# Second token phase of a conv-attention hybrid block: the partner product of q replaced by an exchange matrix on q's fp16 halves

## The reference

```python
# layer 0: attention over channels-first tokens, with a bias table, added to x
x  = x + w_out @ attention(w_qkv @ layernorm_c(x))
# layer 1: attention with relative embeddings, 8 heads of width 32
proj = layernorm(t) @ W + b                 # q, k, v of each head
qk = einsum('bhqd,bhkd->bhqk', q, k)
emb = sinusoidal_embeddings(length, 32)[q - k + length - 1]
qe = einsum('bhqd,qkd->bhqk', q, emb)
weights = softmax((qk + qe) / sqrt(32))
t = t + weights @ v
# layer 2: gates by sinkhorn, top-k routing to 8 experts
t = t + experts(layernorm(t))
```

## Time and profile before

| | us |
|---|---|
| median of 3 runs | 2913.53 (2912.02 to 2914.46) |
| profiled execution | 2905.21 |
| its span | 2903.4 |
| PE busy | 2553.8 (88%) |
| DVE busy | 2023.3 (70%) |
| POOL busy | 1971.1 (68%) |
| ACT busy | 1401.9 (48%) |

### The profile page before, as it was taken

How to read it: one execution, slowest core, us unless ns; L and a number is a source line. 1 busy time by engine, 2 the same in 40 slices (tenths; PEclk the granted TensorE clock), 3 DMA queues, 4 the chain that set the end, 5 groups by cost and what they waited for, 6 DMA issues and landing times. The chain is left out here.

```text
span 2903.4 us, 47732 instructions
## 1 busy us (share of the span) xinstructions
PE 2553.8 (88%) x18726; PEld 872.9 (30%) x18726; DVE 2023.3 (70%) x3094; ACT 1401.9 (48%) x2558; POOL 1971.1 (68%) x767
## 2 busy tenths in 40 slices
PE   6899999999999999879989999999999999761355
PEld 2563222222222222245542222222222222240244
DVE  3575877878878778757766777777777777578134
ACT  4345555555555555422225555555555555440012
POOL 2124888888888888743447887878878878630763
PEclk8999999999999999989999999999999999875568
DMA  3993123221122211268654222223212232260347
GB/s 81 253 227 120 49 49 78 62 52 49 48 74 66 52 48 49 53 230 266 218 184 110 48 63 48 63 80 77 63 48 63 62 90 53 89 188 9 91 122 243
DMA packets 239569, 284.41 MB, mean 98 GB/s; under 512 B 65014, under 2 KB 172790, under 8 KB 236014
## 3 DMA queue, kind: packets, MB, share of 16 engines
q1 hardware_dynamic: 228848, 256.12, 32.5%
q0 software_dynamic: 6144, 16.85, 1.9%
q10 hardware_dynamic: 4352, 8.39, 0.8%
HBM read 171.59 MB, written 110.47 MB: 97 GB/s over the span
## 5 line engine op out<-in xcount | busy, mean ns | idle before, releaser
L843 POOL TENSOR_TENSOR room_af<-room_af 128x2048 f32<-128x2048 f32 x160 | 725.7, 4536 | 164.4 <-ACT room_af L815 150.2
L1191 POOL TENSOR_TENSOR bias<-bias 128x2048 f32<-128x2048 f32 x160 | 724.6, 4529 | 148.5 <-ACT bias L1163 134.6
L978 DVE TENSOR_REDUCE row_min_kf<-PS 128x1 f32<-128x1024 f32 x532 | 627.5, 1220 | 267.4 <-PE PS L970 265.9
L625 DVE CUSTOM_DVE_ANT_0 PS<-PS,bias 128x1024 f32<-128x1024 f32 x532 | 644.2, 1241 | 161.3 <-PE PS L613 148.3
L1163 ACT ACTIVATE bias<-PS 128x512 f32<-128x512 f32 x1024 | 557.1, 597 | 412.2 <-PE PS L1089 411.1
L815 ACT ACTIVATE room_af<-PS 128x512 f32<-128x512 f32 x1024 | 555.7, 595 | 398.2 <-PE PS L737 398.2
L1089 PE MATMUL PS<-stacks_kf 128*128 128x512 f16 x2048 | 533.1, 383 | 7.7 <-PEq L86 7.6
L730 PE MATMUL PS<-QS_af,KS_af 128*128 128x512 f16 x1024 | 334.1, 387 | 11.1 <-PEq L86 4.5
L1089 PEld LDWEIGHTS PS<-stacks_kf 128*128 128x128 f16 x2048 | 156.9, 97 | 448.3 <-ACT bias L1163 292.3
L763 PE MATMUL PS<-room_af,V_af 128*32 128x512 f32 x2048 | 272.7, 605 | 0.3 <-ACT room_af L815 0.3
L1109 PE MATMUL PS<-bias,V_kf 128*32 128x512 f32 x2048 | 272.7, 604 | 0.0
(11 more groups left out here) (180 smaller groups left out, 2847.0 us busy)
## 6 DMA issues: line engine op xcount, KB each, us to landing
stacks_kf<-query_key_halves SPq DMA_DIRECT2D x119, 256.0 KB, 7.0
query_key_halves<-bias SPq DMA_DIRECT2D x32, 768.0 KB, 3.8
query_key_halves<-room_af SPq DMA_DIRECT2D x32, 512.0 KB
KS_af<-query_key_halves SPq DMA_DIRECT2D x51, 256.0 KB, 4.9
QS_af<-query_key_halves SPq DMA_DIRECT2D x51, 256.0 KB, 6.9
V_kf<-values SPq DMA_DIRECT2D x9, 1024.0 KB, 10.5
V_af<-values SPq DMA_DIRECT2D x17, 512.0 KB, 8.9
stacks_kf<-query_key_halves SPq DMA_DIRECT2D x68, 128.0 KB, 9.1
```

The lines of the kernel that those rows point to most:

```text
L625: nc.vector.tensor_tensor_reduce(out=max_ps[n % len(max_ps)], in0=max_ps[n % len(max_ps)], in1=bias_h[:, g * HG + j, z:z + N], scale=-1.0, ...
L843: nc.gpsimd.tensor_tensor(acc[:, u % 2], so_far, prob[:, n % PR], ALU.add).then_inc(acc_ok, 1)
L978: nc.vector.tensor_reduce(row_min[:, m:m + 1], max_ps[n % len(max_ps)], AX.X, ALU.min).then_inc(max_read, 1)
L1191: nc.gpsimd.tensor_tensor(acc[:, u % 2], so_far, prob[:, n % PR], ALU.add).then_inc(acc_ok, 1)
```

## The change

PE makes the partner of q no longer from the layer-normed tokens but from q's own halves in `stg`: two matmuls with a 128x128 exchange matrix `swap` as weights, one for the high and one for the low half, in place of six. Since those halves hold the bias, DVE's step for part 1 of the rotation multiplies only (`tensor_tensor` in place of `scalar_tensor_tensor`). PE must wait for both halves of q of the group. The order of a round is changed, so that other steps stand between q and its partner. `w1_p` shrinks to 3C columns, the bias table `bcol` to four columns, and the four weight jobs for w1q take 256, 256, 512 and 512 columns. DVE writes `swap` in the setup by two copies out of the identity.

```diff
--- before.py
+++ after.py
@@ -61,13 +61,14 @@
 
         wqkv_p = sb("wqkv_p", [P, 2, KT, 3 * C], F16)
         wout_p = sb("wout_p", [P, 2, KT, C], F16)
-        w1_p = sb("w1_p", [P, 2, KT, 4 * C], F16)
+        w1_p = sb("w1_p", [P, 2, KT, 3 * C], F16)
         gate_p = sb("gate_p", [P, 2, KT, E], F16)
         gates = sb("gates", [P, B * NT * E], F32)
         idf = sb("idf", [P, P], F32)
         ones = sb("ones", [P, P], F32)
         bvb = sb("bvb", [P, C], F32)
-        bcol = sb("bcol", [P, 6], F32)
+        bcol = sb("bcol", [P, 2 * G], F32)
+        swap = sb("swap", [P, P], F16)
         eps = sb("eps", [P, 1], F32)
         eyes = sb("eyes", [P, W], F16)
         bias = sb("bias", [P, H, ZU * W], F32)
@@ -166,9 +167,8 @@
                     bc = [("bc", c, 0)] if c < NCH else []
                     qk = [("qk", u, m) for m in range(NQ)] if u >= 0 else []
                     v = [("v", u, m) for m in range(NV)] if u >= 0 else []
-                    last_qk = NQ - 1
                     steps = (qk[0:2] + tp + qk[2:] + v[0:1] + bc + v[1:],
-                              qk[0:3] + proj + qk[3:last_qk] + tp + qk[last_qk:] + v[0:1] + bc + v[1:])[kind]
+                              qk[0:1] + qk[2:3] + proj + qk[1:2] + qk[3:4] + tp + qk[5:6] + qk[4:5] + v[0:1] + bc + v[1:])[kind]
                     some = [("max", n, job) for n, job in jobs[:PER]] if u > early.after else []
                     jobs = jobs[len(some):]
                     for n, name in enumerate(steps):
@@ -336,11 +336,18 @@
                                     pe.wait_ge(high, u + 1)
                                     pe.wait_ge(low, u + 1)
                                 w, g = m % (NQ // G), m // (NQ // G)
-                                last = product(ps, wp, w * C + g * P, lambda s, k: (xh, xl)[s][:, u % 2, k, :])
+                                if kind == 1 and w == 1:
+                                    s = u * G + g
+                                    pe.wait_ge(q_high, 2 * s + 1)
+                                    pe.wait_ge(q_low, 2 * s + 1)
+                                    for h in range(2):
+                                        last = nc.tensor.matmul(ps, swap[:], stg[:, u % 2, g, h, :], start=(h == 0), stop=(h == 1))
+                                else:
+                                    last = product(ps, wp, (w != 0) * C + g * P, lambda s, k: (xh, xl)[s][:, u % 2, k, :])
                             else:
                                 for t in range(2):
                                     last = tokens_first(u, ps[:, t * C:(t + 1) * C],
-                                                        slice((2 * m + t) * P, (2 * m + t + 1) * P), NQ // G * C)
+                                                        slice((2 * m + t) * P, (2 * m + t + 1) * P), 2 * C)
                             last.then_inc(full, 1)
 
                     @block.scalar
@@ -381,7 +388,7 @@
                                 elif w != 1:
                                     act.wait_ge(full, n + 1)
                                     nc.scalar.activation(stg[:, u % 2, g, 2 * w, :], bank(name), ACT.Identity,
-                                                         bias=bcol[:, w * G + g:w * G + g + 1]).then_inc(q_high, 1)
+                                                         bias=bcol[:, w // 2 * G + g:w // 2 * G + g + 1]).then_inc(q_high, 1)
                                 if kind == 1 and m == NQ // G:
                                     turned_high(u, 0)
                             elif what == "v" and kind == 0:
@@ -484,16 +491,15 @@
                                     nc.vector.scalar_tensor_tensor(out=lo, in0=bank(name), scalar=(QS, 1.0)[w] / SC, in1=hi,
                                                                    op0=ALU.mult, op1=ALU.subtract).then_inc(q_low, 1)
                                     continue
-                                b_ = bcol[:, w * G + g:w * G + g + 1]
+                                b_ = bcol[:, w // 2 * G + g:w // 2 * G + g + 1]
                                 if w < 2:
                                     dve.wait_ge(full, n + 1)
                                     if s >= 2:
                                         dve.wait_ge(added, s - 1)
                                     tok = place(u)[1]
                                     if w == 1:
-                                        nc.vector.scalar_tensor_tensor(out=tf[:, s % 2, 1, :], in0=bank(name), scalar=b_,
-                                                                       in1=rots[:, 1, tok], op0=ALU.add,
-                                                                       op1=ALU.mult).then_inc(turned, 1)
+                                        nc.vector.tensor_tensor(tf[:, s % 2, 1, :], bank(name), rots[:, 1, tok],
+                                                                ALU.mult).then_inc(turned, 1)
                                 if w != 1:
                                     dve.wait_ge(q_high, 2 * s + w // 2 + 1)
                                     nc.vector.scalar_tensor_tensor(out=lo, in0=bank(name), scalar=b_, in1=hi, op0=ALU.add,
@@ -1220,7 +1226,7 @@
                 def ssem(name):
                     return es.enter_context(nc.semaphore(name))
 
-                w_sum = KT * (3 * C + C + 4 * C)
+                w_sum = KT * (3 * C + C + 3 * C)
                 room, keys, queries = early.rooms[0], *early.scratch
                 chunks, w_st = room[:, 0:4 * KT * CH], room[:, 4 * KT * CH:4 * KT * CH + w_sum + 256]
                 rel = zf[0:2, 0:SIDE * SIDE]
@@ -1237,7 +1243,7 @@
 
                 WL = []
                 off = 0
-                for src, dst, cols in ((wqkv, wqkv_p, 3 * C), (wout, wout_p, C), (w1q, w1_p, 4 * C)):
+                for src, dst, cols in ((wqkv, wqkv_p, 3 * C), (wout, wout_p, C), (w1q, w1_p, 3 * C)):
                     WL.append((src, dst, w_st[:, off:off + KT * cols].rearrange("p (k n) -> p k n", k=KT)))
                     off += KT * cols
                 small = w_st[:, off:off + 256]
@@ -1252,7 +1258,7 @@
                 cen = room[:, first:first + 2 * P].rearrange("p (i n) -> p i n", i=2)
 
                 WJ = []
-                for n, cols in ((2, slice(0, CH)), (2, slice(CH, 2 * CH)), (0, slice(0, CH)), (0, slice(CH, 3 * C))):
+                for n, cols in ((2, slice(0, C)), (2, slice(C, 3 * C)), (0, slice(0, CH)), (0, slice(CH, 3 * C))):
                     scale = -QS * W1S if n == 2 and cols.start == 0 else (WS, WS, W1S)[n]
                     for k in range(KT):
                         WJ.append((WL[n][1], WL[n][2], k, cols, scale, n == 0))
@@ -1374,8 +1380,11 @@
                                 dve.wait_ge(cst_in, 48)
                                 with nc.allow_low_precision(reason="each sum has a single one among zeros"):
                                     nc.vector.reduce_sum(eyes[:], bass.AP(idf, W - 1, [[P, P], [-1, W], [W, ROWS]]), AX.X)
-                                nc.vector.tensor_scalar(bcol[:, 0:4], bcol[:, 0:4], -QS * W1S, None, ALU.mult)
-                                nc.vector.tensor_scalar(bcol[:, 4:6], bcol[:, 4:6], W1S, None, ALU.mult)
+                                nc.vector.tensor_scalar(bcol[:, 0:G], bcol[:, 0:G], -QS * W1S, None, ALU.mult)
+                                nc.vector.tensor_scalar(bcol[:, G:2 * G], bcol[:, G:2 * G], W1S, None, ALU.mult)
+                                halves_of = [t_.rearrange("p (h t d) -> p h t d", t=2, d=D // 2) for t_ in (swap[:], idf[:])]
+                                for t in range(2):
+                                    nc.vector.tensor_copy(halves_of[0][:, :, t, :], halves_of[1][:, :, 1 - t, :])
                             if j == len(WJ):
                                 dve.wait_ge(w_high, len(WJ) + 1)
                                 nc.vector.scalar_tensor_tensor(out=wout_p[:, 1], in0=WL[1][2], scalar=WS, in1=wout_p[:, 0],
@@ -1892,10 +1901,8 @@
 
     w1 = a["L1_attn_W"].reshape(C, H, 3, D)
     b1 = a["L1_attn_b"].reshape(H, 3, D)
-    swap = np.concatenate([np.arange(D // 2, D), np.arange(D // 2)])
-    w1q = con(np.concatenate([w1[:, :, 0].reshape(C, C), w1[:, :, 0][:, :, swap].reshape(C, C),
-                              w1[:, :, 1].reshape(C, C), w1[:, :, 2].reshape(C, C)], axis=1))
-    cols = [b1[:, 0].reshape(-1, 128), b1[:, 0][:, swap].reshape(-1, 128), b1[:, 1].reshape(-1, 128)]
+    w1q = con(np.concatenate([w1[:, :, i].reshape(C, C) for i in range(3)], axis=1))
+    cols = [b1[:, 0].reshape(-1, 128), b1[:, 1].reshape(-1, 128)]
     b1cols = con(np.concatenate(cols, axis=0).T)
     b1v = con(b1[:, 2].reshape(-1))
```

## The result

| us | before | after |
|---|---|---|
| median of 4 timed runs each | 2912.93 (2912.02 to 2914.46) | 2893.52 (2891.83 to 2896.32) |
| profiled execution | 2905.21 | 2896.32 |
| its span | 2903.4 | 2894.5 |
| PE busy | 2553.8 | 2541.5 |

The account below looks back on a forecast made before the run. A loop from `bc` to `bc` through PE, ACT and DVE was taken as the bound: 14 rounds x 1.52 = 21.3 us, last rounds 0, setup 1.7, together 23.0, so 2913.5 becomes 2890.5 us; own range 2886 to 2896, 8-in-10 range 2885 to 2899.

Parts of the forecast that it names:

- The loop: Second token phase, `bc` to `bc` through PE, ACT and DVE: rounds 17.15 to 15.63 and 15.59 to 14.07, 21.3 us.
- leg 2: From m3's end to the next `bc`, set by DVE: L494 for m4 leaves it, 6.67 to 6.01 us.
- leg 1: PE's work from `bc` to m3's end: m1 sheds 0.86 us, 10.48 to 9.62.
- PE's sum as the bound: Rival, second token phase: PE's wait doesn't grow and both matmul savings count, 29.3 us with setup, 2884.2; chance 0.07.
- The saving hidden: Rival, first leg: DVE's sequence sets it, m1's 0.86 becomes a PE wait, only 0.66 a round counts, 2902.6; chance 0.07.
- The clock falls in each round: Rival, second token phase: PE's longer wait lowers the clock in each of 16 rounds, 3.4 us slower, 2916.9; chance 0.04.
- DMA holds the early rounds: Rival, around 1320: full queues keep four rounds from shortening, 6.1 us lost, 2896.6; chance 0.11.
- ACT and POOL: Second token phase: m4's chain and group 1's store end some 2 us later, entries behind used over a round later: 0.
- the setup: Weight jobs before the token phases: two jobs of 256 columns instead of 512 save 0.85 each, 1.7 us.
- The last two rounds: End of second token phase, without `proj` or transposes: gain 1.4 against loss 1.2 or so, counted 0, 1.5 either side.

Follow-up runs that it names:

- the kernel with three waits in each: Changed kernel with the old order of a round, the exchange product directly behind q: 2933.63 us, 1.0077 of the kernel before.
- the kernel with all three edits: Changed kernel with second-attention loads spread, 512-column weight jobs first and token loads issued ahead of the waiting stores: 2886.71 us, 0.9922 of the kernel before.
- the loads ahead alone: Changed kernel with only the second attention's token loads issued earlier, ahead of the stores waiting for POOL: 2895.14 us, 0.9950 of the kernel before.

## Why the prediction was right, and where it was not

**The loop: right.** A round has 15.63 and 14.07 us as worked out. PE's wait ahead of `bc` is 1.47 where 1.51 was forecast, `swap`'s pair 0.43 as taken from `proj`, and no exchange of rounds 0 to 13 waits (all 1.7 us that PE waits ahead of L344 lie in the last two). The two halves of the term were tried apart. The order alone gave 14.93 and 16.49, 0.66 less each: leg 2. The exchange adds the other 0.86: leg 1. The Trainium skill's 131 ns (TensorE: Matmul & The Clock Gate, Back-to-back issue gap) is not seen in any run here: exchange and products keep 0.216 us, the step that another section of that page (Wait — 56ns, not 53.3ns?) gives for the warm array.

**The rivals.** *PE's sum as the bound* would have had the wait ahead of `bc` not grow, and it grew. *The saving hidden* is refuted by the same rounds: 1.52 is more than 0.66. *The clock falls in each round* isn't so: it is 1.00 through the 14.07 and 15.63 us rounds, and through the 18.20 us rounds of the kernel with three waits in each. The Trainium skill's rule on short idle times with cycling PSUM banks (the same page, A second HAM failure mode: psum-queue depth-cycling) isn't borne out by one wait of 1.5 us a round, nor by three of 0.6 to 1.8. *DMA holds the early rounds* is true in part. I gave it 0.11 and four rounds of 1.52 each. It was one round and 4.3 us, since a fall of the clock went with the hold; and not because that round couldn't be shortened, but because the change itself moved a load.

**The step that failed: "ACT and POOL".** It says that m4's chain ends some 2 us later, with it the store of group 1, and that what is queued behind it on SP is used more than a round later: 0. The first half is right: against `bc`, the store is issued 2.9 us later. The second is wrong, because among what is queued behind are the first loads of the second attention, and these are needed in the next round, the one with the DMA share at 1.07. Their lead fell from 19.4 to 14.7 us where they take 17.9. The wait of 3.12, plus half of the 5.8 us in which PE then worked at 1.2 GHz (1338.7 to 1344.5), less the wait ahead of `bc` that is gone (1.47), makes 4.6; the round shows 4.3. The lead was there to be read in the trace of before, from one row of SP and one of PE: the last of the eleven loads landed there at 1329.4, 2.8 us ahead of the need, and the change takes 4.7 of the lead.

**The term that was mis-sized: the setup.** Forecast -1.7, "and if the clock rises later for lack of columns, half a us or less". It was a loss. Over all profiles the eighth weight job is reached at 41.5 to 42.8 in the four with the jobs of before (mean 42.3), at 43.2 to 46.4 in the six with the narrow ones first (44.9), and at 40.4, 40.6 and 42.8 in the three with a wide one first. So the change costs 2.6 there, and would gain 1.0 with the other order. I had priced the rise of the clock as if it could move only by a fraction of one job, where everything up to the rise, steps of the network too (1.73 against 0.95), runs at half speed. DVE's copies for `swap` took 0.28 for both, below the bound.

**The last two rounds.** Forecast 0 with 1.5 to either side, from a gain of 1.4 and a loss of 1.2. They gave 0.3 (31.32 for 31.64), and nothing between the second profiles of the two kernels (31.31 for 31.27), so the term is 0 as forecast. The waits ahead of the exchanges were 1.7 in sum, for the 2.0 worked out. The changed kernel's rows:

```profile
1501.57 0.59 PE L344 MATMUL PS<-bias,swap 128*128 128x512 f16 x2 [0.72 <-ACT bias L390]
...
1505.21 0.59 PE L344 MATMUL PS<-bias,swap 128*128 128x512 f16 x2 [0.46 <-DVE bias L505]
```

**The sum.** 21.3 became 18.1 (the hold +4.3, the last rounds -0.3, and the phase's start and the rest -0.8 in sum). The setup's -1.7 became +2.6. That leaves 15.5, and the two attentions and the tail add 2.2 (two profiles, and no part of the change accounts for it): 17.7 for the medians' 19.4, whose interval is 13.4 to 20.1 us. The forecast was right in its main term and too high by what the hold and the setup cost. That the result lies so near is in part luck. The two errors come to 8.6 us (4.3 for the hold, and 4.3 from -1.7 to +2.6), and 5.0 us that no step of the prediction worked out went the other way: 1.1 in the phase, 2.2 in the attentions and the tail, 1.7 between profiles and medians. With the two errors alone the gain would be 14.4 and the time 2898.5, just inside the range.

**What stays open.** Whether the narrow jobs cost more than the 2.6 us in the setup: the six kernels with these jobs first come to the first attention at 254.6 to 262.5 us (mean 259.1), the seven others at 250.4 to 258.3 (253.8), 5.3 apart, of which 3.0 stand at the eighth weight job already, and the rest is less than the first token phase scatters. Whether the kernel with all three edits beats the changed one by more than the runs can tell: the two never ran on one chip. Their ratios to before are 0.9922 (0.9907 to 0.9938) and 0.9942 (0.9931 to 0.9954) or 0.9955 (0.9941 to 0.9969).

## What to carry to other kernels

A wait that returns every round is a loop: split it at two instructions into legs, charge every saved or moved instruction to the leg it lies on, and the round comes out to some hundredths of a us. Then look at what the faster round does to things that have a fixed length: for the one-time loads beside it, compare how long they take with the time from their issue to their need, in the new order and the new pace, and don't call anything "used more than a round later" before every entry of the queue is listed. Where the clock is still to rise, the work that stands first counts double, and its shape can be worth more than its amount.

## What the runs showed of the hardware beyond the expected

- **With PE busy throughout, the clock rises earlier or later by which weight jobs stand first.** PE has no pause from 5.8 us to the rise in any of the kernels. With fp32 weight jobs of 512 columns first, the clock first rises at 23.2 to 29.6 us (seven profiles), with those of 256 first at 30.5 to 37.2 (six). Through the network's first twenty matmuls (eighteen with 2 rows of weights, two with 64), 15.1 us without a pause, it stays at the lower level. The Trainium skill (TensorE: Matmul & The Clock Gate, What's actually happening) has the clock follow how busy PE has been; that alone doesn't tell the two groups apart.
- **SP's issuing slows where the queues are crowded.** The store L246 takes SP 0.54 us to issue in the median round of the changed kernel, and 3.25 us at 1336.91, in the round with a DMA share of 1.07. In the kernel before it was 2.76 once, in this row, and with the loads ahead alone 7.81 (at 1319.56):

```profile
1328.36 2.76 SPq L246 DMA_DIRECT2D values<-vst  x1
```

  The rows of the pair L243 (5.23, 7.45 and 8.65) are no such times, since SP waits for group 1's halves between the two: those of the 7.45 row were issued at 1309.99 and 1317.08, in 0.36 us each. Every later entry is held by a slow one, whoever needs it, which fits that two of the edits only moved the wait. No run shows apart that the fullness is the cause.
- **A wait for a load was followed by a slow stretch, shorter waits in each round mostly were not.** Where PE waited for a load in the stretch of full queues, the clock fell to its lower level around the end of the wait: for 6.8 us with waits of 3.12, 3.20, 5.21 and 6.31 us, for 3.4 us with 1.80, 2.38, 2.60, 2.93 and 3.07. The exchange's waits of 1.82 and 1.44, which came back in every round of 18.2 us, were followed by no fall. The length alone doesn't decide: a wait of 2.12 ahead of an exchange in that same kernel was followed by 3.4 us at the lower level (from 1309.3), and the wait of 2.13 ahead of the changed kernel's second `bc` (1270.94) by none. No run tells why.
- **Executions differ most where nothing was changed, and again by a load.** The first token phase has 207.6 to 216.0 us over 13 profiles. In every one of them PE waits for the first attention's early loads, 4.3 to 9.3 us; the rows of the kernel before and of the changed one:

```profile
122.80 0.60 PE L613 MATMUL PS<-KM_af,QM_af 32*128 32x512 f16 x2 [5.89 <-DMA QS_af<-query_key_halves]
...
130.29 0.60 PE L619 MATMUL PS<-KM_af,QM_af 32*128 32x512 f16 x2 [8.61 <-DMA QS_af<-query_key_halves]
```

  Take from the phase's length all of PE's idle time in it and half of the time that PE worked at the lower clock, and 176.9 to 177.2 us are left in all 13 (worked out from the traces). Between these two profiles, PE idles 2.8 us more and works 8.4 us more at the lower level, half of which is 4.2: the whole difference of 7.0. Why the load is later in one execution than in another stays open. Against this, the second token phase of the changed kernel repeats to 0.1 us (265.5 twice). The kernel before has medians of 2911.8, 2895.2 and 2908.7 us on three chips.
